# More buffers for loaded blocks and turned output in an adaLN and mixture-of-experts kernel, and a smaller descriptor scratch

## The chip, the cores and the metric

One core of a Trainium2 chip runs the whole program. The time is device microseconds of one execution. The core has five engines that run their own instruction streams in order and meet through semaphores: TensorE (PE, matrix products; PEld is its weight load), VectorE (DVE), ScalarE (ACT), GpSimd (POOL) and SyncE (SP, which here only issues transfers). ACT and POOL issue transfers too; ACTq, POOLq and SPq name an engine's queue of issues in the rows.

## The reference

4096 tokens of 1024 channels go through two layers. Each layer has a conditioning (a scan over the sequence in both directions) whose output feeds a feed-forward part, and a residual sum. Cut to what matters:

```python
# both layers: base = sigmoid(r) * num / den, with num and den from exponentials scanned over the sequence both ways
x = x + (cond0(x, side) @ (weight * scale[:, None]).T + bias)
h = rmsnorm(cond1(x, side)) * norm_w
logits = h @ router_w.T;  top 4 of 32 experts, softmax weights
routed = sum over the chosen experts of  (silu(h @ w1_gate) * (h @ w1_up)) @ w2
shared = silu(h @ sg) * (h @ su) @ sd
x = x + cond1(x, side) + routed + shared
```

## The kernel before

The program has three stages.

In the first, 32 units (4 sequences by 8 blocks of 128 channels) are scanned one after the other by DVE and ACT. A unit leaves two blocks of 128 by 1024 in memory outside the core: `gated_dram`, the input of the first layer's product, and `ratio_dram`, the second layer's conditioning without its sigmoid.

In the second, the tokens are worked on in 8 halves of 512, here called half 0 to half 7. A half has 32 steps, and a step is one product on PE of 24 matrix operations of 128 by 512. Steps 0 to 15 hold the 8 products of the linear layer of this half (at `STEP_L`) and the 8 down products of the shared expert of the half before (at `STEP_D`). Steps 16 to 31 hold the gate and up products of this half. The halves start after 8 units are done, and from there each engine's stream is written so that the pieces of work of step `i`, the function `fill(h, i, ...)`, stand between the pieces of a scan unit. Units run beside halves 0 to 5; halves 6 and 7 have no unit beside them. Every engine has its own `fill`, all have the same numbering of steps, and what stands in it is in a fixed order. The order is written out by tables at the top of the file (`STEP_L`, `COPY_AT`, `TURN_AT`, `C_LOAD` and others).

In the third stage the tokens are gathered by expert, 149 tiles of 128 rows, multiplied, weighted and added to the output by indirect transfers of POOL (`gather_rows`, `add_rows`), some 17.7 us a tile.

What the change touches lies in the second stage:

- `load_cl` (SP) brings the 8 gated blocks of the next half into the buffers RL. ACT copies each (L821, the high part) and DVE subtracts (L1239, the low part, semaphore `c_lo`). Load `c` waits until the buffer is read.
- `load_rl` (SP) brings the 8 ratio blocks into the same buffers RL. DVE multiplies each with a sigmoid (L1291, semaphore `c1`).
- There are two buffers RL, so load `n` waits for the reader of load `n - 2`.
- The output: DVE adds the down product to the residual (L1248, into OV), PE turns the block (`out_by_token`, L1493, into one bank), ACT copies the bank to RS (`out_copy`, L768), and SP stores RS (`store_out`, L468). There is one RS, so copy `o` waits until store `o - 1` has landed. The copies of the 8 blocks stand at steps 6, 8, 10, 12, 14, 15, 17 and 18 of the next half.
- At step 15, behind copy 5, ACT's stream has the logarithm and exponential of the mean square (L793, L795). At step 16 DVE makes the root of them (L1253, L1257, L1259, L1261) and normalises the blocks (L1270); PE turns each (L1477) and multiplies it with the router (L1479). PE's stream has the turning of output block 5 at step 14, of block 6 at the end of step 15, and L1477 behind that.

SP's stream is one queue: for each step it first has the piece of weights for three steps ahead (L396), then loads of input, ratio and gated blocks and stores, each behind its own waits.

Of the kernel before, what the change touches and what calls it, by code (L numbers as in the profile page):

```python
# [8 lines left out]
P = 128  # L9
# [9 lines left out]
UNITS_PER_HALF = BLOCKS // HALVES  # L19
STEPS = FILLS_PER_UNIT * UNITS_PER_HALF  # L20

ROUTED_TILES = TOK * TOPK // P + EXPERTS
# [44 lines left out]
def copy_step(o):  # L67
    return COPY_AT[o]


# [20 lines left out]
def adaln_moe(nc, x_t, side_t, cond, w_all, u_all, lin_sb, norm_w, router_t, shared_w, expert_w, out):  # L91
# [12 lines left out]
    with ctx:  # L104
# [38 lines left out]
        Z0, Z1, SQ, RS, OV, R, SG, XL0, XL1, RL0, RL1 = (work[:, part0 + i * HALF:part0 + (i + 1) * HALF] for i in range(11))  # L143
        XL, RL, Z, T = [Z0, Z1, XL0, XL1], [RL0, RL1], [Z0, Z1], SQ

# [58 lines left out]
        for name in (  # L204
            "k_in x_in ramp consts_in cond_in kc ek ekv euk h_fwd h_edge h_bwd h_all den g_ln g_inv nf n_edge nb "
            "wv_done num num_w newton1 newton2 sig_steps sig_x gated gated_raw ratio ratio_out gated_out "
            "split_hi split_lo split_pe chunk product read_out c_hi c_lo sig1_steps sig1 c1 z sq z_hi z_lo res "
            "z_tr logits sums z_copy z_out mean r_ln r_exp newton_r r_set l_copy l_tr l_acc silu_steps silu_sig "
            "a_hi_s a_lo_s o_tr o_copy o_out prep prep_act masks rt rt_act rt_mask rt_pe cnt_copy "
            "fill_set fill_out add_idx_set apart entry_ready listed_in slots_in cols_set w1_hi w1_lo w2_hi w2_lo w1_read w2_read "  # L210
            "rows_in row_idx_set x_tr x_hi x_lo silu_done act_done a_tr a_hi a_lo y_hi y_lo y_out zero_set "
            "zero_out"
        ).split():
            s[name] = sem(name)
# [3 lines left out]
        ONE_AHEAD = (  # L218
            "o_tr o_copy o_out gated w1_lo w2_lo num ratio ratio_out gated_out a_tr w1_read w2_read act_done x_lo y_lo y_hi"
        ).split()  # L220
        piece_sem = [[sem(f"piece_in{i}_{j}") for j in range(2)] for i in range(SLOTS)]
        raw_sem = [sem(f"raw_in{m}") for m in range(4)]
        split_sem = [sem(f"split_out{m}") for m in range(4)]
        rl_sem = [sem(f"rl_in{i}") for i in range(2)]
        put_sem = [sem(f"put_out{i}") for i in range(PUTS)]
# [18 lines left out]
        def cl_arrived(h, c):  # L244
            return (h * CB + (c // 2 + 1)) * 16

        def rl_arrived(h, o):
            return (h * CB + (CB // 2 + o // 2 + 1)) * 16

# [127 lines left out]
        def _(sp):  # L377
# [30 lines left out]
            def load_cl(h, c):  # L408
                rows, cols = half_rows(h, c)
                if c < 2:  # L410
                    wait(sp, "c1", (h - 1) * CB + (CB - 2 + c + 1))
                else:
                    wait(sp, "c_lo", h * CB + (c - 1))
                sp.wait_ge(s["gated_out"], ((h // 2) * CB + (c + 1)) * 16 + 1)
                sp.dma_start(RL[c % 2], gated_dram[rows, cols]).then_inc(rl_sem[c % 2], 16)

            def load_rl(h, o):
                rows, cols = half_rows(h, o)
                if o < 2:
                    sp.wait_ge(s["c_lo"], h * CB + (CB - 2 + o + 1))  # L420
                else:
                    sp.wait_ge(s["c1"], h * CB + (o - 1))
                if o == 0:
                    sp.wait_ge(s["ratio_out"], (h // 2 + 1) * CB * 16 + 1)
                sp.dma_start(RL[o % 2], ratio_dram[rows, cols]).then_inc(rl_sem[o % 2], 16)

# [38 lines left out]
            def store_out(h, o):  # L465
                sp.wait_ge(s["o_copy"], h * CB + (o + 2))
                to = out[ds(h * HALF, HALF), o * P:(o + 1) * P].rearrange("(t p) c -> p t c", p=P)
                sp.dma_start(to, RS.rearrange("p (t c) -> p t c", c=P)).then_inc(s["o_out"], 16)  # L468

# [63 lines left out]
        def _(pool):  # L533
# [106 lines left out]
        def _(sc):  # L640
# [134 lines left out]
            def fill(h, i, first, prev, next_):  # L775
# [37 lines left out]
                if next_:  # L813
                    for c in range(CB):
                        if i == (C_HIGH_ALONE if before_all(h) else C_HIGH)[c]:
                            sc.wait_ge(rl_sem[c % 2], cl_arrived(h + 1, c))
# [4 lines left out]
                            sc.activation(chi[:, c * HALF:(c + 1) * HALF], RL[c % 2], ACT.Copy).then_inc(s["c_hi"], 1)  # L821
                if final(h, HALVES - 2) and i == 2 * CB + 6:
# [99 lines left out]
        def _(ve):  # L922
# [313 lines left out]
            def split_c_lo(h, c):  # L1236
                ve.wait_ge(s["c_hi"], h * CB + (c + 1))
                part = slice(c * HALF, (c + 1) * HALF)
                ve.tensor_tensor(clo[:, part], RL[c % 2], chi[:, part].bitcast(f32), ALU.subtract).then_inc(s["c_lo"], 1)  # L1239

# [33 lines left out]
            def fill(h, i, first, prev, next_):  # L1274
# [7 lines left out]
                if not before_all(h):  # L1282
# [4 lines left out]
                    for o in range(CB):  # L1287
                        if i == step_l(o) + 2:
                            ve.wait_ge(s["sig1"], h * CB + (o + 1))
                            ve.wait_ge(rl_sem[o % 2], rl_arrived(h, o))  # L1290
                            ve.tensor_tensor(C1[o], SG, RL[o % 2], ALU.mult).then_inc(s["c1"], 1)  # L1291
                        if prev and i == step_d(o) + 1:
# [87 lines left out]
            def opening(g):  # L1380
                gate_up(g, 0)
                split_x(g + 1)
                gate_up(g, 1)
                ve.wait_ge(s["o_out"], 16 * HALVES * CB + 1)

# [301 lines left out]
```

## Time and profile before

| | |
|---|---|
| median of 3 runs | 4682.92 us (4679.94 to 4685.01) |
| profiled execution, first to last instruction | 4682.9 us |
| PE busy | 4475.7 us, 96% |
| DVE busy | 2567.2 us, 55% |
| ACT busy | 1789.8 us, 38% |
| POOL busy | 722.8 us, 15% |
| stores of turned output, 64 of 256 KB, issue to landing | 5.5 us (median) |
| gathers of expert rows, 151, issue to landing | 4.4 us (median) |
| PE's mean granted clock | 0.979 of full speed |

The profile is one execution. A row of a timeline gives the start and length of an instruction, its engine and line, what it writes and reads, and in brackets how long its engine sat idle before it and what ended that. From 415 us on PE is busy nearly throughout. DVE is busy at over 90% from 400 to 1500 us; from 1600 us, without scans, it is busy less than half of the time. The share of an engine says nothing of a single stage: what a wait costs is read where it ends last.

### The profile page before, as it was taken

The page shows a single profiled execution, that of the slowest core. Times are in us where ns is not written, and L with a number is a line of the kernel's source. Part 1 is how long each engine was busy: PE and PEld are TensorE (multiplying, and loading weights), DVE is VectorE, ACT ScalarE, POOL GpSimd, SP SyncE. Part 2 cuts the span into 40 slices and gives each one's busy share as a digit, 9 for nine tenths or more (in the row PEclk, how much of TensorE's full clock was granted, in tenths as well). Part 3 has the DMA queues.
Part 4 walks back from the last instruction along what each step waited for, and adds up shares of the span by engine and source line. Part 5 has one row for each costly group of instructions (what it writes and reads, how often), then busy time and mean ns, then how long its engine had stood idle before and what let it go on. Part 6 is the DMA issues. An engine that isn't in the chain of part 4 may idle for free.

```text
span 4682.9 us, 60901 instructions
## 1 busy us (share of the span) xinstructions
PE 4475.7 (96%) x19862; PEld 3545.7 (76%) x19863; DVE 2567.2 (55%) x2765; ACT 1789.8 (38%) x2596; POOL 722.8 (15%) x934
## 2 busy tenths in 40 slices
PE   6777999999999999999999999999999999999998
PEld 2245877777777877878888888888888888888887
DVE  8999999999999653433233434444341253333432
ACT  5665555555555333232222323334231142222321
POOL 1000000000000017211111112112111121111111
PEclk8888999999999999999999999999999999999999
DMA  6675767767676766754344545555552254444543
GB/s 226 235 263 184 274 241 268 251 223 282 240 268 226 270 212 190 251 182 111 95 131 112 170 112 160 171 166 150 182 168 57 61 186 145 112 112 116 161 109 61
DMA packets 247928, 835.08 MB, mean 178 GB/s; under 512 B 28160, under 2 KB 61056, under 8 KB 222976
## 3 DMA queue, kind: packets, MB, share of 16 engines
q1 hardware_dynamic: 172944, 572.77, 34.5%
q0 software_dynamic: 47728, 160.07, 15.5%
q10 hardware_dynamic: 27136, 100.67, 5.8%
q8 instruction: 72, 1.18, 0.1%
q14 instruction: 48, 0.39, 0.0%
HBM read 652.40 MB, written 181.01 MB: 178 GB/s over the span
## 4 chain that ended last, share of the span: by engine, by line
PE 80%; DVE 10%; issue 4%; ACT 3%; DMA 2%; POOL 0%; ACTq 0%; DVEq 0%; POOLq 0%; SPq 0%
PE ps L1593 34%; PE ps L1457 22%; PE ps L1607 16%; PE ps L1526 3%; PE ps L1479 1%; PE ps L1582 1%; DVE work L969 1%; DVE work L975 1%; DMA work<-rows_dram,row_idx 1%; PE ps L1477 1%; PE ps L1467 1%; DVE work L996 1%; DVE work L998 1%; DVE work L972 1%; DVE work L1002 1%
## 5 line engine op out<-in xcount | busy, mean ns | idle before, releaser
L1593 PE MATMUL ps<-halves 128*128 128x512 f32 x7152 | 1698.6, 393 | 3.5 <-DVE halves L1356 2.8
L1593 PEld LDWEIGHTS ps<-halves 128*128 128x128 f32 x7152 | 1338.5, 189 | 279.9 <-DVE halves L1356 3.1
L1457 PE MATMUL ps<-halves 128*128 128x512 f32 x6144 | 1450.2, 395 | 13.7 <-issue 12.5
L1457 PEld LDWEIGHTS ps<-halves 128*128 128x128 f32 x6144 | 1154.1, 189 | 287.2 <-issue 47.8
L1607 PE MATMUL ps<-halves 128*128 128x512 f32 x3576 | 834.9, 389 | 1.3 <-DVE halves L1372 1.3
L1607 PEld LDWEIGHTS ps<-halves 128*128 128x128 f32 x3576 | 671.1, 188 | 140.9 <-DVE halves L1372 1.6
L1356 DVE TENSOR_TENSOR halves<-ps,halves 128x1024 fp32r<-128x1024 f32 x150 | 183.7, 1225 | 905.2 <-ACT halves L852 905.2
L1351 DVE TENSOR_TENSOR halves<-work,halves 128x1024 fp32r<-128x1024 f32 (+1 forms) x320 | 440.2, 1433 | 83.6 <-ACT halves L856 83.3
L852 ACT ACTIVATE halves<-ps 128x1024 fp32r<-128x1024 f32 x150 | 154.0, 1027 | 862.4 <-PE ps L1593 862.4
L576 POOL DMA_INDIRECT out<-work,add_idx x149 | 249.8, 1677 | 1417.3 <-DVE work L1378 1382.2
L856 ACT ACTIVATE halves<-work 128x1024 fp32r<-128x1024 f32 (+1 forms) x320 | 369.1, 1229 | 67.0 <-PE ps L1607 56.5
L1372 DVE TENSOR_TENSOR halves<-ps,halves 128x256 fp32r<-128x256 f32 x298 | 112.4, 419 | 491.7 <-ACT halves L884 491.7
L595 POOL TENSOR_SCALAR work<-work 128x1024 f32<-128x1024 f32 x33 | 106.5, 3226 | 1419.9 <-DMA work<-side_t 1419.9
L884 ACT ACTIVATE halves<-ps 128x256 fp32r<-128x256 f32 x298 | 98.5, 382 | 544.4 <-PE ps L1582 544.4
L1378 DVE TENSOR_SCALAR work<-ps,acc 128x512 f32<-128x512 f32 x149 | 111.6, 749 | 276.4 <-PE ps L1607 266.5
L890 ACT ACTIVATE work<-ps,acc 128x512 f32<-128x512 f32 x149 | 102.1, 685 | 408.5 <-PE ps L1607 388.5
L566 POOL DMA_INDIRECT work<-rows_dram,row_idx x151 | 152.5, 1010 | 123.4 <-POOL row_idx L562 69.0
L1526 PE MATMUL ps<-ident,work 128*128 128x128 f32 x1200 | 157.6, 275 | 12.4 <-DMA work<-rows_dram,row_idx 12.4
L975 DVE TENSOR_TENSOR_SCAN work<-decay,edge_in,work 128x1024 f32<-128x1024 f32 x64 | 154.2, 2409 | 14.2 <-ACT edge_in L680 14.2
L1435 PE MATMUL ps<-plain,ident 128*128 128x512 f32 x128 | 83.0, 736 | 73.6 <-ACT halves L735 73.6
L983 DVE TENSOR_TENSOR_SCAN work<-decay,edge_in,work 128x1024 f32<-128x1024 f32 x64 | 150.7, 2355 | 0.0
L1526 PEld LDWEIGHTS ps<-ident,work 128*128 128x128 f32 x1200 | 137.1, 142 | 13.4 <-DMA work<-rows_dram,row_idx 13.3
(186 smaller groups left out, 3674.4 us busy)
## 6 DMA issues: line engine op xcount, KB each, us to landing
halves<-split_dram SPq DMA_DIRECT2D x512, 512.0 KB, 5.6
work<-expert_w SPq DMA_DIRECT2D x192, 1024.0 KB, 5.5
split_dram<-halves ACTq DMA_DIRECT2D x32, 1024.0 KB, 4.9
plain<-shared_w SPq DMA_DIRECT2D x32, 512.0 KB, 3.2
gated_dram<-work ACTq DMA_DIRECT2D x32, 512.0 KB, 4.1
work<-side_t ACTq DMA_DIRECT2D x32, 512.0 KB, 5.6
work<-x_t ACTq DMA_DIRECT2D x32, 512.0 KB, 3.7
ratio_dram<-work ACTq DMA_DIRECT2D x32, 512.0 KB, 4.2
```

The source lines that it names most:

```text
L566: pool.indirect_dma_start(hx, None, rows_dram[:, :], bass.IndirectOffsetOnAxis(row_idx[:, :].bitcast(u32), 0)).then_inc(s["rows_in"], 16)
L576: pool.indirect_dma_start(out[:, :], bass.IndirectOffsetOnAxis(add_idx[:, :].bitcast(u32), 0), y, None, compute_op=ALU.add).then_inc(s["y_ ...
L852: sc.activation(xhi, ps_xt[:, :], ACT.Copy).then_inc(s["x_hi"], 1)
L856: sc.activation(whi[q][:, part], staged(q, part), ACT.Copy).then_inc(s["w1_hi" if q < 4 else "w2_hi"], 1)
L975: ve.tensor_tensor_scan(F[:, ::-1], d, F[:, ::-1], edge_in[:, 0:1], ALU.mult, ALU.add).then_inc(s["h_bwd"], 1)
L983: ve.tensor_tensor_scan(G[:, ::-1], d, G[:, ::-1], edge_in[:, 1:2], ALU.mult, ALU.add).then_inc(s["nb"], 1)
L1351: ve.tensor_tensor(wlo[q][:, part], staged(q, part), whi[q][:, part].bitcast(f32), ALU.subtract)\
L1356: ve.tensor_tensor(xlo, ps_xt[:, :], xhi.bitcast(f32), ALU.subtract).then_inc(s["x_lo"], 1)
L1457: last = pe.matmul(bank(k % 4), w, op[:, part], start=(c == 0 and w is w_hi and op is hi), stop=(c == CB - 1 and w is w_lo))
L1526: last = pe.transpose(ps_xt[:, c * P:(c + 1) * P], hx[:, c * P:(c + 1) * P], ident[:, :])
L1593: last = pe.matmul(ps_h[:, a * 512:a * 512 + 512], xp[:, xk * P:(xk + 1) * P], wp[:, rhs], start=(xk == 0 and xp is xhi and wp is whi[q]), ...
L1607: last = pe.matmul(ps_y[:, h * 512:h * 512 + 512], ap_[:, (q * 2 + k) * P:(q * 2 + k + 1) * P], wp[:, rhs:rhs + 512], start=(q == 0 and k ...
```

## The change

The buffers RL become four, the two new ones and a second RS lying in a new tensor `more` of 1536 columns. Load `n` of gated or ratio blocks waits for the reader of load `n - 4`. The four loads have a semaphore each. Output copy `o` goes to RS for even `o` and to RS1 for odd `o`, each with a semaphore of its own, and waits for store `o - 2`; the first two copies wait for none. The ratio loads get a step by a function of its own: loads 0 and 1 in step 0, 2 and 3 in step 1 (before: 0 in step 0, 1 in step 1, 2 and 3 in steps 2 and 3), and load `o` from 4 on in step `STEP_L[o - 4] + 3`, which is 3, 4, 5 and 7 (before: 4, 6, 8 and 10). The steps of the gated loads stay. The scratch for descriptors of the transfers that POOL issues is set to 4096 bytes a partition.

```diff
+def ratio_step(o):
+    return STEP_L[o - 4] + 3 if o >= 4 else o // 2
...
-        XL, RL, Z, T = [Z0, Z1, XL0, XL1], [RL0, RL1], [Z0, Z1], SQ
+        more = sb("more", 3 * HALF)
+        RL2, RL3, RS1 = (more[:, i * HALF:(i + 1) * HALF] for i in range(3))
+        XL, RL, Z, T = [Z0, Z1, XL0, XL1], [RL0, RL1, RL2, RL3], [Z0, Z1], SQ
+        RS_OF = [RS, RS1]
...
-        rl_sem = [sem(f"rl_in{i}") for i in range(2)]
+        rl_sem = [sem(f"rl_in{i}") for i in range(4)]
+        out_sem = [sem(f"o_out{i}") for i in range(2)]
+        OUT_ALL = HALVES * CB // 2 * 16
...
             def load_cl(h, c):
-                if c < 2:
-                    wait(sp, "c1", (h - 1) * CB + (CB - 2 + c + 1))
+                if c < 4:
+                    wait(sp, "c1", (h - 1) * CB + (CB - 4 + c + 1))
                 else:
-                    wait(sp, "c_lo", h * CB + (c - 1))
+                    wait(sp, "c_lo", h * CB + (c - 3))
...
             def load_rl(h, o):
-                if o < 2:
-                    sp.wait_ge(s["c_lo"], h * CB + (CB - 2 + o + 1))
+                if o < 4:
+                    sp.wait_ge(s["c_lo"], h * CB + (CB - 4 + o + 1))
                 else:
-                    sp.wait_ge(s["c1"], h * CB + (o - 1))
+                    sp.wait_ge(s["c1"], h * CB + (o - 3))
...
-                        if i == (step_l(o - 2) + 2 if o >= 2 else o):
+                        if i == ratio_step(o):
                             load_rl(h, o)
...
             def out_copy(h, o):
                 sc.wait_ge(s["o_tr"], h * CB + (o + 2))
-                sc.wait_ge(s["o_out"], (h * CB + o) * 16 + 1)
-                sc.activation(RS, OUT_BANK, ACT.Copy).then_inc(s["o_copy"], 1)
+                if h or o >= 2:
+                    sc.wait_ge(out_sem[o % 2], (h * (CB // 2) + o // 2) * 16)
+                sc.activation(RS_OF[o % 2], OUT_BANK, ACT.Copy).then_inc(s["o_copy"], 1)
...
-            pool.wait_ge(s["o_out"], 16 * HALVES * CB + 1)
+            pool.wait_ge(out_sem[0], OUT_ALL)
+            pool.wait_ge(out_sem[1], OUT_ALL)
...
-    nc = bacc.Bacc("TRN2", target_bir_lowering=False, num_devices=1)
+    nc = bacc.Bacc("TRN2", target_bir_lowering=False, num_devices=1, dynamic_dma_scratch_size=SCRATCH)
```

The stream of ACT at steps 14 to 16 of half 1, before. `o_out` counts the stores, `o_tr` the turned blocks, `sums` the sums of squares.

```order
L660 ACTIVATE work<-work 128x1024 [waits kc]
L768 ACTIVATE work<-ps 128x512 [waits o_out,o_tr] x2
L793 ACTIVATE work<-ps,eps 128x512 [waits sums]
L795 ACTIVATE work<-work 128x512 [waits r_ln]
L730 DMA ratio_dram<-work 128x1024 [waits ratio]
```

And in the changed kernel, where the line numbers are higher by 12 to 14:

```order
L673 ACTIVATE work<-work 128x1024 [waits kc]
L782 ACTIVATE work<-ps 128x512 [waits o_out0,o_tr]
L782 ACTIVATE more<-ps 128x512 [waits o_out1,o_tr]
L807 ACTIVATE work<-ps,eps 128x512 [waits sums]
L809 ACTIVATE work<-work 128x512 [waits r_ln]
L743 DMA ratio_dram<-work 128x1024 [waits ratio]
```

The instructions stand in the same order; the two copies, of blocks 4 and 5, write different buffers and wait for different counters.

The stream of SP at steps 0 to 2 of half 1, before. `halves<-split_dram` are weight pieces, `work<-x_t` the input blocks.

```order
L433 DMA work<-x_t 128x512 [waits l_tr]
L425 DMA work<-ratio_dram 128x512 [waits ratio_out,c_lo]
L433 DMA work<-x_t 128x512 [waits l_tr]
L396 DMA halves<-split_dram 128x1024 [waits chunk,split_out0]
L396 DMA halves<-split_dram 128x1024 [waits product]
L425 DMA work<-ratio_dram 128x512 [waits c_lo]
L433 DMA work<-x_t 128x512 [waits res] x2
L396 DMA halves<-split_dram 128x1024 [waits chunk,split_out1]
L396 DMA halves<-split_dram 128x1024 [waits product]
L425 DMA work<-ratio_dram 128x512 [waits c1]
```

And in the changed kernel:

```order
L445 DMA work<-x_t 128x512 [waits l_tr]
L437 DMA work<-ratio_dram 128x512 [waits ratio_out,c_lo]
L445 DMA work<-x_t 128x512 [waits l_tr]
L437 DMA work<-ratio_dram 128x512 [waits c_lo]
L408 DMA halves<-split_dram 128x1024 [waits chunk,split_out0]
L408 DMA halves<-split_dram 128x1024 [waits product]
L445 DMA work<-x_t 128x512 [waits res]
L437 DMA more<-ratio_dram 128x512 [waits c_lo]
L445 DMA work<-x_t 128x512 [waits res]
L437 DMA more<-ratio_dram 128x512 [waits c_lo]
L408 DMA halves<-split_dram 128x1024 [waits chunk,split_out1]
L408 DMA halves<-split_dram 128x1024 [waits product]
```

Ratio load 1 has moved ahead of the piece of step 1, loads 2 and 3 ahead of the piece of step 2, and loads 1 to 3 now all wait for `c_lo`, the splits of the gated blocks.

## Rows read from the trace of the kernel before

**Rows 1.** Waits of PE: line waited for, us in total, times, longest us.
```profile
PE ps L1477 <- DVE work L1270: 31.6, 9, 11.9
...
PE ps L1526 <- DMA work<-rows_dram,row_idx: 12.4, 4, 3.6
```

**Rows 2.** Waits of DVE.
```profile
DVE work L1253 <- ACT work L793: 9.4, 4, 3.9
```

**Rows 3.** Waits of ACT.
```profile
ACT work L768 <- DMA out<-work: 136.1, 27, 9.3
```

**Rows 4.** Timeline of half 4: start, length, engine, line, what it does.
```profile
1225.90 1.28 DVE L1002 SCALAR_TENSOR_TENSOR work<-work,neg_gain 128x1024 f32<-128x1024 f32 x1
...
1227.93 0.69 DVE L1253 TENSOR_SCALAR work<-ps 128x512 f32<-128x512 f32 x1 [0.75 <-ACT work L793]
...
1226.72 0.60 ACT L768 ACTIVATE work<-ps 128x512 f32<-128x512 f32 x1 [5.66 <-DMA out<-work]
...
1228.02 0.60 PE L1493 MATMUL ps<-ident,work 128*128 128x128 f32 x4
1231.72 1.12 PE L1477 MATMUL ps<-ident,work 128*128 128x128 f32 x4 [3.11 <-DVE work L1270]
```

**Rows 5.** Timeline of half 5.
```profile
1436.22 0.69 DVE L1253 TENSOR_SCALAR work<-ps 128x512 f32<-128x512 f32 x1 [0.83 <-ACT work L793]
...
1440.01 1.12 PE L1477 MATMUL ps<-ident,work 128*128 128x128 f32 x4 [3.18 <-DVE work L1270]
```

**Rows 6.** Timeline of half 6: PE, ACT, DVE.
```profile
1634.15 0.60 PE L1493 MATMUL ps<-ident,work 128*128 128x128 f32 x4
...
1640.92 0.60 PE L1493 MATMUL ps<-ident,work 128*128 128x128 f32 x4
1644.37 1.11 PE L1477 MATMUL ps<-ident,work 128*128 128x128 f32 x4 [2.85 <-DVE work L1270]
...
1639.37 0.60 ACT L768 ACTIVATE work<-ps 128x512 f32<-128x512 f32 x1 [9.30 <-DMA out<-work]
...
1635.94 0.75 DVE L1306 SCALAR_TENSOR_TENSOR work<-work,lsb,plain 128x512 f32<-128x512 f32 x1
1640.58 0.69 DVE L1253 TENSOR_SCALAR work<-ps 128x512 f32<-128x512 f32 x1 [3.89 <-ACT work L793]
```

**Rows 7.** Timeline of half 7: DVE, PE.
```profile
1844.08 0.69 DVE L1253 TENSOR_SCALAR work<-ps 128x512 f32<-128x512 f32 x1 [3.92 <-ACT work L793]
...
1847.87 0.66 PE L1477 MATMUL ps<-ident,work 128*128 128x128 f32 x4 [2.51 <-DVE work L1270]
```

**Rows 8.** Timeline of half 2, PE.
```profile
814.77 1.11 PE L1477 MATMUL ps<-ident,work 128*128 128x128 f32 x4 [2.26 <-DVE work L1270]
```

**Rows 9.** Stretches behind the wait; busy PE, PEld, DVE, ACT, POOL, granted clock, DMA.
```profile
815.00:818.00 3.00, 3.00 (x8) 1.00 (x8) 2.42 (x4) 1.49 (x3) 0.00 (x0) 0.51 0.50 169
...
1231.70:1237.50 5.80, 5.78 (x12) 1.80 (x12) 4.03 (x6) 2.86 (x5) 0.00 (x0) 0.50 0.23 79
...
1644.30:1647.20 2.90, 2.83 (x6) 0.89 (x6) 2.71 (x5) 1.74 (x3) 0.00 (x0) 0.50 0.23 68
...
1847.80:1852.50 4.70, 4.63 (x12) 1.46 (x12) 3.98 (x7) 2.86 (x5) 3.48 (x5) 0.64 0.29 92
```

**Rows 10.** POOL's scatters and gathers by line: shortest, median, longest issue in ns.
```profile
L576 POOL DMA_INDIRECT out<-work,add_idx x149: 1570/1588/5017, 2049.4 to 4670.5; - x149
...
L566 POOL DMA_INDIRECT work<-rows_dram,row_idx x151: 957/1010/1027, 1940.8 to 4651.7; - x151
```

**Rows 11.** Timeline around one long scatter.
```profile
2882.24 1.01 POOL L566 DMA_INDIRECT work<-rows_dram,row_idx  x1 [0.79 <-POOL row_idx L562]
...
2895.08 1.04 PE L1526 MATMUL ps<-ident,work 128*128 128x128 f32 x8
...
2896.32 4.48 DVE L1351 TENSOR_TENSOR halves<-work,halves 128x2048 fp32r<-128x2048 f32 x2
...
2897.34 4.92 POOL L576 DMA_INDIRECT out<-work,add_idx  x1 [8.37 <-DVE work L1378]
```

More of the change, by code:

```diff
@@ L20 @@
 STEPS = FILLS_PER_UNIT * UNITS_PER_HALF
+ALONE = 2 * UNITS_PER_HALF
+SCRATCH = 4096
 ROUTED_TILES = TOK * TOPK // P + EXPERTS
@@ L208, in adaln_moe @@
             "z_tr logits sums z_copy z_out mean r_ln r_exp newton_r r_set l_copy l_tr l_acc silu_steps silu_sig "
-            "a_hi_s a_lo_s o_tr o_copy o_out prep prep_act masks rt rt_act rt_mask rt_pe cnt_copy "
+            "a_hi_s a_lo_s o_tr o_copy prep prep_act masks rt rt_act rt_mask rt_pe cnt_copy "
             "fill_set fill_out add_idx_set apart entry_ready listed_in slots_in cols_set w1_hi w1_lo w2_hi w2_lo w1_read w2_read "
@@ L218, in adaln_moe @@
         ONE_AHEAD = (
-            "o_tr o_copy o_out gated w1_lo w2_lo num ratio ratio_out gated_out a_tr w1_read w2_read act_done x_lo y_lo y_hi"
+            "o_tr o_copy gated w1_lo w2_lo num ratio ratio_out gated_out a_tr w1_read w2_read act_done x_lo y_lo y_hi"
         ).split()
@@ L244, in cl_arrived @@
         def cl_arrived(h, c):
-            return (h * CB + (c // 2 + 1)) * 16
+            return (h * (CB // 2) + (c // 4 + 1)) * 16
         def rl_arrived(h, o):
-            return (h * CB + (CB // 2 + o // 2 + 1)) * 16
+            return (h * (CB // 2) + (CB // 4 + o // 4 + 1)) * 16
         def before_all(h):
@@ L409, in load_cl @@
                 rows, cols = half_rows(h, c)
-                if c < 2:
-                    wait(sp, "c1", (h - 1) * CB + (CB - 2 + c + 1))
+                if c < 4:
+                    wait(sp, "c1", (h - 1) * CB + (CB - 4 + c + 1))
                 else:
-                    wait(sp, "c_lo", h * CB + (c - 1))
+                    wait(sp, "c_lo", h * CB + (c - 3))
                 sp.wait_ge(s["gated_out"], ((h // 2) * CB + (c + 1)) * 16 + 1)
-                sp.dma_start(RL[c % 2], gated_dram[rows, cols]).then_inc(rl_sem[c % 2], 16)
+                sp.dma_start(RL[c % 4], gated_dram[rows, cols]).then_inc(rl_sem[c % 4], 16)
             def load_rl(h, o):
                 rows, cols = half_rows(h, o)
-                if o < 2:
-                    sp.wait_ge(s["c_lo"], h * CB + (CB - 2 + o + 1))
+                if o < 4:
+                    sp.wait_ge(s["c_lo"], h * CB + (CB - 4 + o + 1))
                 else:
-                    sp.wait_ge(s["c1"], h * CB + (o - 1))
+                    sp.wait_ge(s["c1"], h * CB + (o - 3))
                 if o == 0:
                     sp.wait_ge(s["ratio_out"], (h // 2 + 1) * CB * 16 + 1)
-                sp.dma_start(RL[o % 2], ratio_dram[rows, cols]).then_inc(rl_sem[o % 2], 16)
+                sp.dma_start(RL[o % 4], ratio_dram[rows, cols]).then_inc(rl_sem[o % 4], 16)
             def load_xl(h, o):
@@ L467, in store_out @@
                 to = out[ds(h * HALF, HALF), o * P:(o + 1) * P].rearrange("(t p) c -> p t c", p=P)
-                sp.dma_start(to, RS.rearrange("p (t c) -> p t c", c=P)).then_inc(s["o_out"], 16)
+                sp.dma_start(to, RS_OF[o % 2].rearrange("p (t c) -> p t c", c=P)).then_inc(out_sem[o % 2], 16)
             def unit(u, par, fill, summed_by_pe=False):
@@ L815, in fill @@
                         if i == (C_HIGH_ALONE if before_all(h) else C_HIGH)[c]:
-                            sc.wait_ge(rl_sem[c % 2], cl_arrived(h + 1, c))
+                            sc.wait_ge(rl_sem[c % 4], cl_arrived(h + 1, c))
                             if c == 0 and not before_all(h):
@@ L820, in fill @@
                                 sc.wait_ge(s["fill_out"], 16)
-                            sc.activation(chi[:, c * HALF:(c + 1) * HALF], RL[c % 2], ACT.Copy).then_inc(s["c_hi"], 1)
+                            sc.activation(chi[:, c * HALF:(c + 1) * HALF], RL[c % 4], ACT.Copy).then_inc(s["c_hi"], 1)
                 if final(h, HALVES - 2) and i == 2 * CB + 6:
@@ L1238, in split_c_lo @@
                 part = slice(c * HALF, (c + 1) * HALF)
-                ve.tensor_tensor(clo[:, part], RL[c % 2], chi[:, part].bitcast(f32), ALU.subtract).then_inc(s["c_lo"], 1)
+                ve.tensor_tensor(clo[:, part], RL[c % 4], chi[:, part].bitcast(f32), ALU.subtract).then_inc(s["c_lo"], 1)
             def down(h, o, k, hk):
@@ L1289, in fill @@
                             ve.wait_ge(s["sig1"], h * CB + (o + 1))
-                            ve.wait_ge(rl_sem[o % 2], rl_arrived(h, o))
-                            ve.tensor_tensor(C1[o], SG, RL[o % 2], ALU.mult).then_inc(s["c1"], 1)
+                            ve.wait_ge(rl_sem[o % 4], rl_arrived(h, o))
+                            ve.tensor_tensor(C1[o], SG, RL[o % 4], ALU.mult).then_inc(s["c1"], 1)
                         if prev and i == step_d(o) + 1:
@@ L1383, in opening @@
                 gate_up(g, 1)
-                ve.wait_ge(s["o_out"], 16 * HALVES * CB + 1)
+                ve.wait_ge(out_sem[0], OUT_ALL)
+                ve.wait_ge(out_sem[1], OUT_ALL)
             def rest(g, j):
```

## The prediction

> **What bounds the kernel now.** I read the page's shares first, then the waits of each engine, then the timeline of the places where TensorE (PE) waits. PE is busy 96% of the span (the table above), and from about 415 us on it is the engine that everything else follows: eight halves of 512 tokens, then the expert tiles. So only PE's idle time can be won back, and PE's list of waits says how little there is that this change could touch. Its second largest entry is L1477, the turning of the normalised blocks at step 16 of a half, which waits for VectorE's (DVE) L1270: 31.6 us in 9 waits, of which the later seven are worth 2.3 to 3.2 us each. The gathers of the expert tiles follow with 12.4 us in 4 waits [rows 1]. PE records no wait at all for a weight piece, a gated block or a ratio block.
>
> What can the change reach? ScalarE (ACT) sits 136.1 us idle before L768, the copy of a turned output block, in 27 waits for the store of the block before it [rows 3]. ACT is no bound, so these 136 us are not the price. I look for who stands behind ACT. At step 15 the copy of block 5 stands ahead of L793, the logarithm that opens the root of the mean square, and DVE's root (L1253) waits for that. DVE records this wait 4 times, 9.4 us together, at most 3.9 us [rows 2]. That is the whole path from the single output buffer to PE: store of block 4, copy of block 5, L793, L1253 to L1261, L1270, L1477.
>
> **The change part by part.**
>
> *Two buffers for the turned output.* Copy 5 then waits for store 3, which was queued two copies earlier, no longer for store 4. So copy 5 starts when PE has turned block 5. What PE gains in a half is the smaller of how far DVE's root moves forward and how long PE waits.
>
> Half 4: copy 5 starts at 1226.72 after 5.66 us of idle time. DVE ends L1002 at 1225.90 + 1.28 = 1227.18, and L1253 starts at 1227.93, of which 0.75 us is the wait for ACT [rows 4]. DVE has its own work up to 1227.18, so L1253 can move by 0.75 us and no more. PE ends its last work before L1477 at 1228.02 + 0.60 = 1228.62 and waits 3.11 us; 0.75 us of this goes and 2.36 us stays, because DVE is late by its own work. Half 5 is the same picture: 0.83 us of 3.18 us [rows 5].
>
> Half 6: here DVE has no scan work left. Block 5 is turned at 1634.15 + 0.60 = 1634.75, but copy 5 starts at 1639.37, after 9.30 us. DVE is free at 1635.94 + 0.75 = 1636.69 and L1253 starts at 1640.58. From copy 5 to L1253 it is 1640.58 - 1639.37 = 1.21 us, so with the copy at 1634.8 ACT would be ready at 1636.0 and DVE's own 1636.69 decides. From L1253 to L1477 it is 1644.37 - 1640.58 = 3.79 us, so the first block is ready at 1640.5. PE is ready at 1640.92 + 0.60 = 1641.5. The whole 2.85 us go, with 1 us to spare [rows 6]. Half 7 likewise: DVE waits 3.92 us, PE 2.51 us, all of which goes [rows 7].
>
> Halves 1 to 3 gain nothing directly: the four waits worth 0.75 + 0.83 + 3.89 + 3.92 = 9.39 us are all that rows 2 counts, so in the other halves L1253 did not wait for ACT. Half 0 has no output copies. Direct sum: 0.75 + 0.83 + 2.85 + 2.51 = 6.94 us.
>
> *The clock behind the wait.* After the idle time PE runs a while at the lower of its two clock levels, 1.2 GHz where 2.4 is the other. The stretch 1231.7 to 1237.5 shows a granted clock of 0.50, half 6 has 2.9 us at 0.50, half 7 has 4.7 us at 0.64, half 2 has 3.0 us at 0.51 [rows 9]. PE is busy through all four, so what the clock costs is length times what is missing: 5.8 x 0.50 = 2.90 us, 1.45 us, 4.7 x 0.36 = 1.69 us, 1.47 us. Half 5's first transposes take the same 1.12 us as half 4's [rows 4, 5], so I give it 2.90 us too. In halves 6 and 7 no idle time is left and I take the whole of it back: 3.14 us; the bounds are 0 (these are light operations, and the clock may fall on their account) and 3.14. In halves 4 and 5 2.36 us of idle time stays, nearest to half 2's 2.26 us [rows 8], which paid 1.47 us; so 1.43 us comes back in each, 2.86 us together; bounds 0 and 5.80. Clock term: 6.0 us, between 0 and 8.9.
>
> *Four buffers for gated and ratio blocks; the ratio loads earlier in SyncE's (SP) queue.* Nobody on DVE or ACT is recorded as waiting for one of these loads, so having them earlier is worth 0. What the wider buffers free is SP, which stood behind DVE's splits; behind it in the queue stand weight pieces and output stores, for which PE did not wait. Loads 2 and 3 of a half now stand in step 1, ahead of the pieces of later steps, and load 3 waits for the last split of the half before. Before, load 1 stood in the same step with the same wait. So no new wait is in front of a piece; 0, and at worst a piece comes late once in a half, which is a rival below.
>
> *A descriptor scratch of 4096 bytes.* It serves only POOL's transfers. The gathers take 957 to 1027 ns to issue, all 151 of them, so nothing held any; of the scatters the median is 1588 ns and the longest 5017 [rows 10]. There are four long ones, and behind each PE waits once, the 12.4 us of rows 1. If a full scratch made these four, a quarter of the scratch would make four times as many. The row at 2897.34 speaks against it. It lasts 4.92 us, that is 3.34 us more than 1.58, so its work began at 2900.68; DVE's pair of L1351 that started at 2896.32 ended at 2900.80 [rows 11]. The Trainium skill says the same (SBUF — State Buffer, section "SBUF: two separate sides"): a DVE operation with two inputs in SBUF holds the port it shares with GpSimd for its whole length against a GpSimd operation that reads SBUF, and a locked-out GpSimd writes no descriptors. The trace agrees within 0.12 us. By this rule the smaller scratch adds nothing; by the other reading it adds twelve waits. I take 0. The bounds are 0 and 12 x 3.1 = 37 us. In between lies a hold on a gather, which has time: the one of 2882.24 lands some 4.4 us later and PE asks for its rows at 2895.08 [rows 11], so 8 us are spare.
>
> The Trainium skill gives sizes from which a count could be estimated (DMA: Bandwidth & Descriptors, sections "Terms" and "The descriptor swizzle": 16 bytes a descriptor, nine on each engine for a transfer over 128 partitions): 4096 / 16 / 9 is 28 transfers, an estimate. No run here shows it.
>
> Sum: 6.94 + 6.0 = 12.9 us. The profiled execution spans 4682.9 us, with nothing to add around it, and the median of the runs is 4682.92, so I take both as one: 4682.9 - 12.9 = 4670.0 us.
>
> **The rivals.**
> A. Only the idle time goes; the clock falls in the four halves as before, because the turning of blocks is light work. For it: idle times as near as 3.11 us (half 4) and 2.85 us (half 6) left 5.8 us and 2.9 us at the lower level, so idle time alone does not set it [rows 4, 6, 9]. Against it: in half 4 the same light work regains the full clock after 5.8 us. Time 4682.9 - 6.9 = 4676.0.
> B. The gain is taken back in the same place. In halves 6 and 7 the margin is 1 us; and SP's new order may bring a piece late. Were DVE's root to come 1.5 us later than I think in both halves, and one piece late by 1 us in each of seven halves, it would be 4682.9 - 12.9 + 3 + 7 = 4680.
> C. The scratch. If a full scratch holds POOL and a scatter waits for it as the four do, it is 12 more PE waits of 3.1 us: 4670.0 + 37.2 = 4707.2. It decides from the fourth additional hold (4 x 3.1 = 12.4 us eats the gain), and from the eighth the kernel is slower by more than 0.2%. Against it stand the 151 even gathers and the coincidence with DVE.
>
> **How the numbers follow.** Forecast 60%, A 26%, B 8%, C 6%. The predicted time is 4670.0. Its own range is 4667 (all of the clock term) to 4673. A change of less than 0.2%, 9.4 us, can hardly be told from none: the runs before lie within 5.1 us. Faster by over 0.2% means under 4673.5: the forecast without its upper edge and a little of A, 0.59. A and B fall within 0.2%: 0.34. Slower: C and what I have not thought of, 0.07. The range for 8 in 10 takes in A and most of B: 4666 to 4680.5.
>
> **What would show it.** Right: no idle time before the output copy that ends with a store; L1253 without a wait for L793 in all halves; L1477's wait gone in halves 6 and 7 and about 2.4 us in halves 4 and 5, untouched in 1 to 3; granted clock near 1 behind it in halves 6 and 7. Scatters with four long issues, as before. Wrong: a wait in front of L1477 in half 6 or 7 that names another releaser; a clock of 0.5 there though PE did not wait (A); a PE wait for pieces (B); long issues on POOL where DVE runs no L1351 pair, or more than four (C).

## The result, and the profile after

The changed kernel takes 4653.5 us (median of 4 runs, 4646.8 to 4654.4), the kernel before 4681.4 us (4 runs, 4677.4 to 4685.0): a ratio of 0.994, 95% interval 0.9926 to 0.9953. That is 28 us, where 12.9 were forecast and 16.9 (4682.9 - 4666) was the far edge of the range. The profiled execution spans 4651.7 us, so 31.2 us less than that of before. I read that difference first.

The totals of PE: 4475.7 us busy before, 4465.9 now. The work is the same, so the 9.8 us are a faster clock; the other 21.4 us are idle time. One execution says little of the clock: three kernels below whose PE does the same work as before show 4470.0 to 4470.4 us, so some 5 of the 9.8 us may be chance. Where it went is in PE's list of waits (line waited for, us in total, times, longest us). Lines are 12 to 15 higher than before.

After:

```profile
PE ps L1492 <- DVE work L1284: 23.8, 7, 11.9
PE ps L1541 <- DMA work<-rows_dram,row_idx: 12.4, 4, 3.7
PE ps L1472 <- DVE halves L1253: 2.6, 3, 1.0
PE ps L1472 <- issue: 2.5, 3, 1.3
```

Before, the rows of the same list for the products (L1457 is now L1472):

```profile
PE ps L1457 <- issue: 12.5, 5, 3.1
```

The wait before the turning of the normalised blocks fell by 7.8 us and lost two of its nine entries [rows 1]. A second loss fell by as much: 12.5 us in front of products, now 2.6 + 2.5. The forecast did not mention that row. The gathers' waits are unchanged.

Half 6, which before waited 2.85 us [rows 6], and half 7 (the last row), timeline of PE, ACT and DVE after:

```profile
1624.96 0.60 PE L1508 MATMUL ps<-ident,work 128*128 128x128 f32 x4
1625.40 0.60 PE L1492 MATMUL ps<-ident,work 128*128 128x128 f32 x4
...
1618.83 0.60 ACT L782 ACTIVATE more<-ps 128x512 f32<-128x512 f32 x1 [4.72 <-PE ps L1508]
...
1619.99 0.75 DVE L1320 SCALAR_TENSOR_TENSOR work<-work,lsb,plain 128x512 f32<-128x512 f32 x1
1620.66 0.68 DVE L1267 TENSOR_SCALAR work<-ps 128x512 f32<-128x512 f32 x1
...
1824.79 0.60 PE L1492 MATMUL ps<-ident,work 128*128 128x128 f32 x4
```

ACT's copy now waits for PE alone, DVE's root follows DVE's own work without a gap, and PE goes from one turning to the next. Halves 4 and 5 keep the wait that DVE's own scan work causes [rows 4, 5]:

```profile
1219.72 0.66 PE L1492 MATMUL ps<-ident,work 128*128 128x128 f32 x4 [2.26 <-DVE work L1284]
...
1425.21 0.91 PE L1492 MATMUL ps<-ident,work 128*128 128x128 f32 x4 [2.26 <-DVE work L1284]
```

The clock behind it, in stretches of the after trace (us, PE busy, granted clock, DMA share, GB/s), in halves 3 to 7:

```profile
1015.60:1020.00 4.40, 4.40 (x12) 0.61 0.37 126
1219.70:1225.50 5.80, 5.78 (x18) 0.71 0.32 100
1425.20:1431.00 5.80, 5.79 (x18) 0.71 0.32 111
1625.20:1630.00 4.80, 4.80 (x22) 1.00 0.60 165
1824.60:1830.00 5.40, 5.40 (x26) 1.00 0.60 166
```

Before, the same stretches:

```profile
1024.30:1028.70 4.40, 4.12 (x17) 1.00 0.34 113
...
1440.00:1445.80 5.80, 5.79 (x13) 0.50 0.23 79
1644.40:1649.20 4.80, 4.80 (x15) 0.69 0.12 35
1847.90:1853.30 5.40, 5.40 (x17) 0.68 0.25 76
```

In halves 6 and 7 the clock is full at once: 4.8 x 0.31 + 5.4 x 0.32 = 3.2 us. In half 4 (0.50 before, rows 9) and half 5 it is 5.8 x 0.21 = 1.2 us each. Together 5.6 us, against 6.0 in the forecast. Half 3 shows that one stretch alone proves little: it waits 2.61 us in both traces, and its clock was 1.00 before and 0.61 after. The same stretch in every kernel of this document but the last, 5.8 us from the first turning of halves 1 to 7, tells more. With one output buffer the clock costs 6.7 to 12.6 us in the seven stretches together (10.0 on the mean of seven kernels, 12.3 in the kernel before), with two 3.4 to 9.6 us (6.0 on the mean of five, 6.7 in the changed kernel). In halves 6 and 7 it is 1.00 in all ten stretches of the kernels with two buffers, and in five of fourteen with one. So the clock does come back, but 4.0 us is the better figure, and the kernel before was profiled in a poor execution.

Then the loss that I had not looked at. PE's row in front of the first product of half 2, before:

```profile
707.64 3.11 PE L1457 MATMUL ps<-halves 128*128 128x512 f32 x13
713.75 6.43 PE L1457 MATMUL ps<-halves 128*128 128x512 f32 x27 [3.00 <-issue]
```

and after:

```profile
705.65 2.20 PE L1472 MATMUL ps<-halves 128*128 128x512 f32 x9
708.85 7.36 PE L1472 MATMUL ps<-halves 128*128 128x512 f32 x30 [0.99 <-DVE halves L1253]
```

Halves 3, 4 and 5 are alike: 3.06, 2.81 and 2.53 us before, 0.90, 0.76 and 1.29 after, and one step later 1.12 us in half 3 before, 0.63 and 0.61 in halves 3 and 5 after. Together they are the 12.5 and 5.2 us. Halves 1, 6 and 7 have none. Halves 2 to 5 are those whose step 0 lies behind a jump back in PE's stream: its loop runs over halves 1 to 5.

What SP did just ahead of it, before (L415 is a gated load, L396 a weight piece; rows of short stretches, so that single issues show):

```profile
702.05 0.33 SPq L415 DMA_DIRECT2D work<-gated_dram  x1
702.80 0.80 SPq L396 DMA_DIRECT2D halves<-split_dram  x2
703.70 0.37 SPq L396 DMA_DIRECT2D halves<-split_dram  x1
```

and after:

```profile
697.01 0.33 SPq L408 DMA_DIRECT2D halves<-split_dram  x1
699.81 0.33 SPq L408 DMA_DIRECT2D halves<-split_dram  x1
702.45 0.33 SPq L408 DMA_DIRECT2D halves<-split_dram  x1
```

Before, the last gated load of the half held SP until DVE's split, which ended at 702.02, and three piece transfers left within 1.3 us behind it. Now they leave at the pace at which PE frees their slots. SP's own waits for a split (first before, then after) say how general this is:

```profile
SPq L415 <- DVE halves L1239: 250.1, 47, 15.4
```

```profile
SPq L427 <- DVE halves L1253: 23.8, 9, 16.7
```

Last, the end of the program. The last instruction with a row is the last scatter. Before, then after:

```profile
4670.46 1.58 POOL L576 DMA_INDIRECT out<-work,add_idx  x1 [1.38 <-DVE work L1378]
```

```profile
4644.69 1.58 POOL L588 DMA_INDIRECT out<-work,add_idx  x1 [1.38 <-DVE work L1392]
```

From its start to the end of the span it is 4682.9 - 4670.5 = 12.4 us before and 4651.7 - 4644.7 = 7.0 us after. So the 21.4 us of idle time are 7.8 at L1492, 12.5 - 5.1 = 7.4 at step 0, 5.4 at the end, and 0.8 elsewhere. Behind step 0 the clock was 0.83 for 10 us in halves 3 and 4 before and 1.00 in halves 2 to 5 after, which is 2 x 10 x 0.17 = 3.4 us more of the 9.8.

### The profile page after: what moved, and what is told of

Same layout as the page of the kernel before. It is cut to its first block, busy times and chain, and to the rows that moved or that the text cites. A ratio compares the mean times of both kernels' runs of the same rounds, so it can differ in the third digit from the quotient of the medians.

```text
span 4651.7 us, 60897 instructions
## 1 busy us (share of the span) xinstructions
PE 4465.9 (96%) x19862; PEld 3539.9 (76%) x19863; DVE 2565.2 (55%) x2765; ACT 1791.9 (39%) x2596; POOL 731.0 (16%) x934
## 4 chain that ended last, share of the span: by engine, by line
PE 55%; DMA 1%; issue 1%; DVE 1%; ACT 0%; POOL 0%; POOLq 0%; DVEq 0%; ACTq 0%
PE ps L1608 34%; PE ps L1622 16%; PE ps L1541 3%; PE ps L1597 1%; DMA work<-rows_dram,row_idx 1%; PE ps L1472 1%; DVE halves L1365 0%; ACT halves L866 0%; DMA out<-work,add_idx 0%; DVE work L1392 0%; PE ps L1508 0%; POOL acc L573 0%; POOLq L572 0%; POOL out L588 0%; DVE halves L1370 0%
## 5 line engine op out<-in xcount | busy, mean ns | idle before, releaser
L1472 PE MATMUL ps<-halves 128*128 128x512 f32 x6144 | 1444.9, 394 | 6.2 <-DVE halves L1253 2.6
L1472 PEld LDWEIGHTS ps<-halves 128*128 128x128 f32 x6144 | 1150.2, 188 | 278.2 <-issue 36.8
L588 POOL DMA_INDIRECT out<-work,add_idx x149 | 250.1, 1679 | 1417.5 <-DVE work L1392 1217.8
L1541 PE MATMUL ps<-ident,work 128*128 128x128 f32 x1200 | 158.2, 276 | 12.4 <-DMA work<-rows_dram,row_idx 12.4
```

The lines of the kernel that those rows point to most:

```text
L588: pool.indirect_dma_start(out[:, :], bass.IndirectOffsetOnAxis(add_idx[:, :].bitcast(u32), 0), y, None, compute_op=ALU.add).then_inc(s["y_ ...
L1472: last = pe.matmul(bank(k % 4), w, op[:, part], start=(c == 0 and w is w_hi and op is hi), stop=(c == CB - 1 and w is w_lo))
L1541: last = pe.transpose(ps_xt[:, c * P:(c + 1) * P], hx[:, c * P:(c + 1) * P], ident[:, :])
```

## The experiments

Theory S for the second loss: SP is no longer held before gated loads, so pieces do not leave in a burst shortly before PE jumps back. Rival L: the loss at step 0 belongs to the loop and came down by itself. Each kernel was timed against the kernel before on its own chip (4680.2, 4678.5 and 4680.4 us in the three groups).

**Only the second output buffer.** This kernel also has the scratch of 4096 bytes, which makes room for the buffer.

```diff
-        sc.wait_ge(s["o_out"], (h * CB + o) * 16 + 1)
-        sc.activation(RS, OUT_BANK, ACT.Copy)...
+        if h or o >= 2:
+            sc.wait_ge(out_sem[o % 2], (h * (CB // 2) + o // 2) * 16)
+        sc.activation(RS_OF[o % 2], OUT_BANK, ACT.Copy)...
```

> The kernel before with the second output buffer alone (two RL, old ratio steps; the 4 KB scratch is needed to make room for it). Theory S (the unpredicted part of the gain is SyncE's: it no longer stands before gated loads 6 and 7, so weight pieces do not leave in bursts ahead of PE's return to the head of its loop, and PE's idle time at step 0 of halves 2 to 5 shrinks): this kernel has only the output part. PE's wait at L1477 falls from 31.6 to about 24 us and is gone in halves 6 and 7, idle time at step 0 of halves 2 to 5 stays near 12.5 us; 4681.4 - 7.8 - 6 (clock) = about 4668. Rival L (the idle time at step 0 belongs to the loop's return and came down with the output copies or with another start time, not with the loads): idle time at step 0 is about 5 us here already, and the time is about 4656.

Measured: 4663.0 us, ratio 0.9963 (0.9949 to 0.9976). PE's list:

```profile
PE ps L1484 <- DVE work L1276: 24.3, 9, 11.9
PE ps L1464 <- issue: 10.7, 4, 3.0
```

The wait of step 16 falls as in the changed kernel, the loss at step 0 stays. Rival L expected about 5 us there and falls. The time is 5 us better than expected; that is what the end of the program gives (12.4 - 7.1 = 5.3 us), which I had not priced.

**Only the four RL buffers and the ratio steps.** The changed kernel with `out_sem`, `RS_OF` and the condition `h or o >= 2` put back to one `RS` and `o_out`. The scratch of 4096 bytes stays.

> The changed kernel with one output buffer as before: four RL, new ratio steps and the scratch are what is left. Theory S: idle time at step 0 of halves 2 to 5 about 5 us instead of 12.5, with about 3 us of clock behind it; PE's wait for the normalised blocks as before, 31 us; 4681.4 - 7.3 - 3 = about 4671. Rival L: step 0 as before, 12.5 us, and about 4681. The forecast on record took these edits at 0.

Measured: 4666.7 us, ratio 0.9971 (0.996 to 0.9981).

```profile
PE ps L1487 <- DVE work L1280: 33.3, 10, 11.9
PE ps L1467 <- DVE halves L1249: 3.4, 4, 1.2
PE ps L1467 <- issue: 0.3, 1, 0.3
```

The mirror image: step 16 as before, step 0 down to 3.7 us. The edits that the forecast took at 0 are worth this.

**No buffer at all, only SP's order.**

```diff
-C_LOAD = (22, 22, 23, 24, 25, 26, 27, 29)
+C_LOAD = (22, 22, 23, 24, 25, 26, 28, 30)
```

> The kernel before with one edit: gated loads 6 and 7 stand in steps 28 and 30 of SyncE's stream instead of 27 and 29, so each stands behind the weight piece that it held up. No buffer is added. Theory S: the three pieces at the end of a half leave one by one, idle time at step 0 of halves 2 to 5 falls to 5 to 8 us, waits at L1477 stay; about 4673. Rival L: step 0 stays at 12.5 us; about 4681. A third possibility is that load 7 comes too late for ScalarE's copy and DVE's split, which would put a wait of 1 to 3 us for the split before step 0: over 4681.

Measured: 4670.7 us, ratio 0.9978 (0.9969 to 0.9987). SP's issues before step 0 of half 2, and PE there:

```profile
696.04 0.33 SPq L415 DMA_DIRECT2D work<-gated_dram  x1
697.37 0.33 SPq L396 DMA_DIRECT2D halves<-split_dram  x1
700.05 0.33 SPq L396 DMA_DIRECT2D halves<-split_dram  x1
```

```profile
699.63 5.83 PE L1457 MATMUL ps<-halves 128*128 128x512 f32 x25
706.14 6.18 PE L1457 MATMUL ps<-halves 128*128 128x512 f32 x26 [0.69 <-DVE halves L1239]
```

The pieces leave one by one and the loss at step 0 is 3.7 us in all. SP still waits 207.6 us for splits (250.1 before), so it is the two loads next to the jump that count. Two numbers in a table give 9.5 us, about a third of the whole gain. The late load did no harm.

**Four buffers, but the old wait for loads 6 and 7.**

```diff
-                    wait(sp, "c_lo", h * CB + (c - 3))
+                    wait(sp, "c_lo", h * CB + (c - 1 if c >= 6 else c - 3))
```

> The changed kernel in which gated loads 6 and 7 wait for the split of two blocks before, as with two buffers (the four buffers stay). Theory S: SyncE is held again at these two loads, the pieces leave in bursts, idle time at step 0 of halves 2 to 5 is back at 10 to 12.5 us; 4653.5 + 8 = about 4661 to 4664. Rival L: nothing changes, 4653.5, step 0 about 5 us.

Measured: 4663.0 us, ratio 0.996 (0.9946 to 0.9973), 9.5 us above the changed kernel's median (against its own kernel before it gains 17.2 us where the changed kernel gains 27.9). The two intervals just overlap, and the trace decides: `PE ps L1472 <- issue` is back at 10.8 us in 5 waits. So it is these two waits of SP that bring the loss at step 0 back, not the number of buffers or where they lie.

**What PE lacks at step 0.** The kernel before with PE's loop written out.

```diff
-            with pe.Fori(1, HALVES - 2) as h:
+            for h in range(1, HALVES - 2):
                 half(h, False)
```

> The kernel before with one edit: PE's loop over halves 1 to 5 is written out, so PE's stream has no jump back; SyncE's stream and its bursts of pieces stay as they are. Theory F (what PE lacks at step 0 is its own instructions: behind the jump back to the loop's head they are fetched anew, and in the kernel before this comes some 2 us later because of the pieces issued in a burst): the idle time at step 0 of halves 2 to 5, 12.5 us, is gone to 0 to 3 us, some 3 us of clock come back too; 4680.2 - 9.5 - 3 = about 4668. Rival P (a late weight piece or a late split holds the product itself): the 12.5 us stay, and it is 4680.

Measured: 4665.1 us, ratio 0.9971 (0.9961 to 0.998). PE around step 0 of half 2:

```profile
699.71 22.60 PE L1457 MATMUL ps<-halves 128*128 128x512 f32 x99
```

No idle time above 0.25 us at step 0 of any half, though SP's stream is the one with the bursts (three pieces within 1.3 us from 702.35 on). Rival P (data late) falls: the product's operands were there. The page counts the packets of the queue that brings instructions (packets, MB, share), before and here:

```profile
q8 instruction: 72, 1.18, 0.1%
```

```profile
q8 instruction: 60, 0.98, 0.1%
```

Four jumps less are 12 packets of 16 KB less, three for each jump. So behind a jump PE's instructions are brought anew by a transfer. The traces also show when. In half 2 the second of these packets starts at about 710.98 before and 706.07 after (the same row asked for 710.95 to 711.05, and for 706.05 to 706.15):

```profile
q8 instruction: 1, 0.02, 55.4%
```

```profile
q8 instruction: 1, 0.02, 55.2%
```

PE resumes 2.8 us later in both, at 713.75 and 708.85. At all 40 jumps, in the ten kernels here that have the loop, PE resumes 2.7 to 2.9 us after the start of this packet (once 3.2). What differs is when the packet starts. In the six kernels with the burst (the one before, the second output buffer alone, the old wait, and the three that change only the scratch) it starts between 0.6 us before and 0.6 us after PE has run out of work, and PE idles 2.4 to 3.3 us. In the four others it starts 1.0 to 2.2 us before that, and PE idles 0.6 to 1.7 us. So PE waits for its instructions, and with a burst of pieces ahead the packet is some 2 us late.

In half 2 the DMA engines were 98% busy before and 93% after in the 2 us until PE stopped, and 100% and 23% while it stood. That the burst delays the packet by keeping the DMA engines busy is argued from this, not shown.

**The changed kernel, with the loop written out.** The same edit.

> The changed kernel with PE's loop over halves 1 to 5 written out. Theory F: the 5.2 us that are left at step 0 (0.6 to 1.3 us each, put down to DVE's last split or to issue) go nearly all; 4653.5 - 4 = about 4649. Rival P (what is left is the wait for DVE's last split, as the releaser says): about 3 us stay in three halves, 4651 to 4653.

Measured: 4649.2 us, ratio 0.994 (0.9926 to 0.9954). The 5.2 us at step 0 are gone entirely, so the releaser named there (DVE's last split) was not the cause either. The profiled execution spans 4643.4 us and the median is 4.3 us under that of the changed kernel, but against their own kernels before the two gain 29.4 and 27.9 us and the two intervals coincide: the trace shows a gain over it, the times don't.

**The scratch alone.**

```diff
-    nc = bacc.Bacc("TRN2", target_bir_lowering=False, num_devices=1)
+    nc = bacc.Bacc("TRN2", target_bir_lowering=False, num_devices=1, dynamic_dma_scratch_size=4096)
```

> The kernel before with the descriptor scratch of 4096 bytes and no other edit. Theory E (the smaller scratch shortens the program's end: from the issue of the last scatter to the end of the span it is 12.4 us in the kernel before and 12.5 in the one with later gated loads, both with the default scratch, against 7.0 to 7.5 in the four kernels with 4096 bytes): the stretch is about 7.1 us here, nothing else changes, 4680.2 - 5.2 = about 4675. Rival 0 (the forecast on record: the scratch is worth nothing, the shorter end comes from fewer or other transfers): 12.4 us and 4680.

Measured: 4673.4 us, ratio 0.9987 (0.9978 to 0.9996). The last scatter starts at 4665.44 and the span ends at 4672.7: 7.3 us. PE's waits at steps 0 and 16 are like those of before, 11.4 and 32.8 us.

**Other sizes.** The same line with 8192 and 2048.

> The kernel before with a descriptor scratch of 8192 bytes. From the issue of the last scatter to the end of the span: 12.4 us at 16384 bytes (the default, twice seen), 7.0 to 7.5 us at 4096 (eight kernels). Theory E1 (the end takes time in proportion to the scratch, 5.2 us for 12288 bytes): 8.9 us. Rival E2 (a step: any smaller scratch gives the short end): 7.2 us; or 12.4 us if the step lies below.

> The kernel before with a descriptor scratch of 2048 bytes. Theory E1 (in proportion): the end takes 6.3 us. Rival E2 (a step): 7.2 us. At this size the forecast's case C (a full scratch holds POOL) is looked at too: if it exists, scatters or gathers here take longer to issue than the 1.58 and 1.01 us of before, and PE waits for gathered rows more than 4 times; I expect 4 waits as before.

Measured, one run each: 4674.8 and 4671.9 us. The last scatters:

```profile
4664.05 1.58 POOL L576 DMA_INDIRECT out<-work,add_idx  x1 [1.38 <-DVE work L1378]
```

```profile
4662.92 1.58 POOL L576 DMA_INDIRECT out<-work,add_idx  x1 [1.38 <-DVE work L1378]
```

With spans of 4673.1 and 4670.2 us the end takes 9.1 us at 8192 bytes and 7.3 at 2048. So with 12.4, 9.1, 7.3, 7.3 neither theory is right: it falls in proportion down to 4096 and not below. The packets of the last scatter say where. The last one ends 5.6 to 6.2 us after the scatter's start at every size. From there to the end of the span it is 6.7 us in each of the three kernels with 16384 bytes, 3.2 at 8192, 1.4 in each of the eight kernels with 4096, and 1.5 at 2048. So what the scratch shortens lies behind the last transfer, and most of the 7.2 us that stay is the last scatter itself. What the time behind it is spent on, the trace does not show. At 2048 bytes POOL's issues still are

```profile
L576 POOL DMA_INDIRECT out<-work,add_idx x149: 1572/1588/5022, 2042.5 to 4662.9; - x149
L566 POOL DMA_INDIRECT work<-rows_dram,row_idx x151: 957/1010/1027, 1934.1 to 4644.2; - x151
```

with 4 waits of PE for gathered rows: no size tried makes a full scratch hold POOL. POOL's idle time ahead of the scatters, too, is 1417 us before, 1421 at 8192, 1416 at 4096 and 1425 at 2048 bytes.

**The old ratio steps.**

```diff
-    return STEP_L[o - 4] + 3 if o >= 4 else o // 2
+    return STEP_L[o - 2] + 2 if o >= 2 else o
```

> The changed kernel with the ratio loads in the steps in which they stood before (four buffers stay). Theory S: SyncE's freedom before step 0 is what counts, and ratio loads have no one waiting for them, so nothing changes: 4653.5 within 3 us, step-0 idle about 5 us or less. Rival: the earlier ratio loads are part of the gain, and it is slower by 5 us or more, with a new PE wait in steps 0 to 10 of a half.

Measured: 4653.3 us, ratio 0.9947 (0.9934 to 0.9961). The time is that of the changed kernel, as expected. The idle time at steps 0 and 1 is not: 8.2 us instead of 5.2, the largest of it

```profile
918.55 6.77 PE L1472 MATMUL ps<-halves 128*128 128x512 f32 x29 [1.71 <-issue]
```

where the changed kernel has 0.63 us. This too lies behind the jump, and its end comes 2.4 us after the start of a third instruction packet. Whether the ratio steps are worth these 3 us, the times cannot tell.

**What is left at step 16.** The changed kernel with the loop written out, and with the root and the first two normalised blocks moved ahead of DVE's three scan operations, to the end of step 15.

```diff
                     if i == 2 * CB:
-                        root(h)
-                        normalize(h, 0)
-                        normalize(h, 1)
+                        split_z_lo(h, 0)
...
+                    if i == 2 * CB - 1:
+                        root(h)
+                        normalize(h, 0)
+                        normalize(h, 1)
```

> The changed kernel with PE's loop written out, and DVE's root with the first two normalised blocks at the end of step 15 instead of the start of step 16, ahead of three scan operations of 3.8 us. The wait of 2.26 us (2.61 in half 3) that is left at step 16 of halves 1 to 5 comes from these three operations. If so, it goes, 11.7 us with the lower clock behind it 5 us more: 4649.2 - 11.7 - 5 = about 4633. Rival: the scan chain, late by 4.3 us in each half, holds PE's sums of the scan units or the splits of the next half instead, and PE waits there: 4645 to 4650. A second rival: the third block is late in place of the first, and half of the gain stays: 4640.

Measured: 4659.6 us, ratio 0.9954 (0.9941 to 0.9968): 10 us worse than without the move by the medians, 9 by the gains over their own kernels before (20.8 and 29.4). Half 3:

```profile
1013.31 1.05 PE L1496 MATMUL ps<-work,rw 128*32 128x512 f32 x2
1018.33 1.11 PE L1494 MATMUL ps<-ident,work 128*128 128x128 f32 x4 [3.97 <-DVE work L1284]
...
1015.53 0.69 DVE L1248 TENSOR_TENSOR halves<-work,halves 128x512 fp32r<-128x512 f32 x1 [1.15 <-ACT halves L814]
```

The first two blocks come without a wait, and then the third is 3.97 us late instead of the first by 2.61: DVE's scan work still stands in between, and behind it DVE waits for ACT, whose part of the normalised blocks had not been moved. The second rival, worse than I had priced it.

## Why the prediction was wrong

*The output buffer: right in mechanism, and in size partly by luck.* Forecast 6.94 us of idle time and 6.0 of clock. Measured 7.8 and 5.6 in the trace, and by the runs 17.2 - 5.1 = 12.1 us (second output buffer less the scratch alone) against 12.9. Over all kernels the two terms err against each other. PE's wait for the normalised blocks is 32.2 us on the mean of the seven kernels with one output buffer and 24.1 on that of the five with two, so 8.1 us of idle time; the clock behind it is 10.0 and 6.0 us, so 4.0. The sum is again 12.1. The four predicted places behaved as worked out: the waits of halves 6 and 7 gone, 2.26 us left in halves 4 and 5 (forecast 2.36 and 2.35). The idle term was too small because "Halves 1 to 3 gain nothing directly" holds only of the execution that was profiled. In the kernel with the scratch alone, DVE's root waits for ACT in half 2 as well, and PE waits 3.52 us there instead of 2.26:

```profile
809.22 0.69 DVE L1253 TENSOR_SCALAR work<-ps 128x512 f32<-128x512 f32 x1 [1.17 <-ACT work L793]
```

With one output buffer PE's waits at step 16 of halves 1 to 5 sum to 12.7 to 15.3 us (14.1 before), the excess not always in the same halves; with two to 11.7 to 12.4 us (11.7 in the changed kernel). Rival A (only idle time goes) is out: the clock was full behind the vanished waits. Rival B is out too, no piece came late.

*The buffers RL: this step failed.* It said that "behind it in the queue stand weight pieces and output stores, for which PE did not wait", and so took SP's freedom at 0. It is worth 13.5 - 5.1 = 8.4 us (the RL buffers alone less the scratch), and by putting two waits of SP back 9.5 by the medians or 27.9 - 17.2 = 10.7 by the gains. The premise was true and the conclusion wrong. PE waited for no piece; it lost time to `issue` in front of products, 12.5 us in 5 entries of the very list from which rows 1 come, and I passed over that row because it names no releaser. (The sentence "The gathers of the expert tiles follow with 12.4 us" skips it, and two larger rows, L1467 with 26.0 and L1421 with 22.9 us.) What PE waited for were its own instructions behind the jump, which none of the forecast's terms or rivals held. A row of 12.5 us was larger than the direct sum.

*The scratch: this step failed as well.* "I take 0. The bounds are 0 and 12 x 3.1 = 37 us": the lower bound was set to 0 without a reason, since I asked only what the scratch does while POOL uses it. It shortens the end of the program by 5.2 us. The other half of the step held: four long scatters as before, and four waits of PE for gathered rows at every size. The estimate of 28 transfers that was worked out from the Trainium skill would be 14 at 2048 bytes, and nothing was held there either; that a DVE operation holds POOL's issue (SBUF — State Buffer, section "SBUF: two separate sides") stands, with the longest scatter at 5.02 us at 16384, 8192 and 2048 bytes and 5.03 at 4096.

The three parts sum to 12.1 + 8.4 + 5.1 = 25.6 us, near the 28 measured; by the intervals the first is known to some 8 us, the second to 7 and the third to 4. The range for 8 in 10, 4666 to 4680.5, covered only what the output buffer could do; the rivals all lay above the forecast, and none below it.

## What to carry to other kernels

An idle row that names no releaser is still a loss with a cause: before an edit is priced at 0, look at every idle entry of the bounding engine in the stretch that it touches, and ask what recurs with the loop rather than with the data. A queue in order that waits for one transfer sends what stands behind it in a burst; putting the waiting entry one step later can give most of what more buffers give. A size parameter can act where it is not used: here at the end of the program.

## What was not expected of the hardware

A jump back in PE's stream cost 2.5 to 3.1 us of idle PE in halves 2 to 5 of the kernel before, 0.6 to 1.3 us in the changed kernel, where SP's issues ahead of it are spread out, and 0 without the jump, with three instruction packets of 16 KB less per jump. PE resumes 2.7 to 2.9 us after the second of these packets starts, at 39 of 40 jumps. The Trainium skill (Advanced Engine Details and Errata, section "Control Flow Timing") gives about 51 ns for a branch. No idle time measured at a jump here is that short: what PE waits for is the packet, which that figure does not price.

The stretch from the last scatter to the end of the span depends on the descriptor scratch: 12.4 us at 16384 bytes, 9.1 at 8192, 7.3 at 4096 and 2048, of which the part behind the last transfer is 6.7, 3.2, 1.4 and 1.5 us. The Trainium skill (Runtime: NRT & Kernel Launch, section "The ~15µs preamble/postamble breakdown") counts a barrier together with a reset of the DMA rings, about 2 us, among what follows a kernel. What shrinks here is 5.2 us, more than that entry, and that it is this reset no run here shows.
